# Three stages of a graph network kernel run with shorter lags between their steps

## The chip, the cores and the metric

One core of a Trainium2 chip runs the whole program in one launch. The metric is the device time of that launch in microseconds. Lower is better.

## The reference

Fifty thousand nodes of 128 features pass through four graph layers (a two-layer GCN, a three-layer GraphSAGE, an attention layer with a GRU, a summing layer), each followed by a residual sum and a layer norm. The parts that the change touches are these (biases left out):

```python
# GCN, second half: h is the scaled table of the first half
x1 = layernorm(x + dinv * segment_sum(h[src], dst) + ...)
# GraphSAGE, third layer, and what the attention layer asks of its output
x2 = layernorm(x1 + inv_deg * segment_sum(v[src], dst) + rest)
message = x2 @ W_msg + b_msg ;  score = x2 @ W_att ;  gh_n = x2 @ W_hh_n.T
# last layer
x4 = layernorm(x3 + segment_sum(x3[src], dst) @ W_neigh.T + x3 @ W_self.T + b)
```

## The kernel before

The nodes are cut into T = 98 groups of 512. The program is a row of stages, each of which walks over all 98 groups and writes a table to HBM that the next stage reads; every stage ends with a barrier, so the next one starts only when the last store has landed. The stages in question are gcn_second (its tiles are g2_*, shown as g_* in the profile), sage_third (s3_*, shown as s_*) and combine (cb_*).

Inside such a stage every engine runs its own program. `over_groups(eng, [(lag, stage), ...])` writes it: at step s the engine carries out, in the order of the list, each stage for group s - lag. The waits inside a stage block the engine (or the queue of SyncE, "SP", which issues the plain loads and stores), so everything that stands later in the list, or in later steps, stays behind them.

The work on one group g of sage_third is: DVE copies the row indices (`aim`, lag 0); GpSimd issues 3 to 5 indirect gathers of 128 rows each, 4.24 on average; DVE makes the one-hot matrices (`prepare`); PE multiplies rows by one-hots (`sums`); ACT copies the sum (`catch`); PE transposes it (`flip`); ACT scales it (`weight`); DVE adds the row block `s_rest` and takes the statistics (`add`, L1863); ACT takes the root (`root`); DVE inverts it (`invert`); ACT normalises (`apply`); PE transposes (`turn`); ACT copies (`hold`); PE multiplies (`message`), first 2 matmuls for `hx`, then 8 for the messages; ACT copies `hx` (`note`); DVE adds the bias to the messages (`bias`, writes `s_mout` and `s_asks`, L1874 and L1876). gcn_second ends with `apply`, and combine has a `dense` product in place of `flip`. On DVE the lags in the lists count from `prepare`, which itself runs four steps behind `aim`: `on_vector` adds 4 to each.

SP loads and stores for sage_third: `s_rest` (two buffers; the load of group g first waits until `add` of group g - 2 is done), `x2t` (after `hold`), `hxt` (after `note`), `t_m` and `asks_d` (both after `bias`). The store helper and the load helper are:

```python
def load(sp, q, to, what, loaded, free=None, slots=2):
    if free is not None and not (isinstance(q.t, int) and q.t < slots):
        wait_for(sp, free, q.t - (slots - 1))
    sp.dma_start(to, what).then_inc(loaded, 16)

def store(sp, q, to, what, made, stored):
    wait_for(sp, made, q.t + 1)
    sp.dma_start(to, what).then_inc(stored[q.d % len(stored)], 16)
```

The rows that are gathered lie in a ring of eight groups: `aim` of group s waits until `sums` of group s - 6 (or s - 7) is done.

Of the kernel before, what the change touches and what calls it, by code (L numbers as in the profile page):

```python
# [23 lines left out]
BLK = 4  # L24
GRP = BLK * P
T = -(-NODES // GRP)
NPAD = T * GRP
# [156 lines left out]
def build_program(nc, x, src, dst, w1, b1, w2, b2, ws0, wn0, sb0, ws1, wn1, sb1, ws2, wn2, sb2,  # L184
# [782 lines left out]
# [3 lines that stand above are left out]
# [444 lines left out]
    def gcn_second():  # L1414

        with ExitStack() as ctx:
            ph = Phase(ctx, "g2")
            e = EdgeRows(ph, t_h0, D)
            agg = ph.pair("agg", [P, GRP])
            ln = LayerNorm(ph)  # L1420
            rest, z, xout = ph.pair("rest", [P, GRP], n=4), ph.pair("z", [P, GRP], n=4), ph.pair("xout", [P, GRP])
            held, turned = ph.sem("held"), ph.sem("turned")
            loaded, added, stored = ph.sems("loaded", 4), ph.sem("added"), ph.sems("stored")
            scaled, weighted = ph.pair("scaled", [P, GRP]), ph.sem("weighted")
            block = ctx.enter_context(nc.Block())

            @block.gpsimd
            def _(pool):
                e.fetch(pool)

            @block.sync
            def _(sp):
                over_groups(sp, [
                    (3, lambda q: load(sp, q, rest[q.r][:, :], group_of(r1, q.t), loaded[q.r], added, 4)),
                    (9, lambda q: store(sp, q, group_of(t_x1[0:NPAD, :], q.t), xout[q.u][:, :], ln.applied,
                                        stored))])
                all_stored(sp, stored)

            @block.tensor
            def _(pe):  # L1440
                def sums(q):
                    e.fetched(pe, q)
                    if not is_first(q.t):
                        pe.wait_ge(held, q.t - 1)
                    e.sum_by_feature(pe, q, [bank[q.u]]).then_inc(e.summed, 1)

                def turn(q):
                    pe.wait_ge(held, q.t + 1)
                    if not is_first(q.t):
                        pe.wait_ge(weighted, q.t - 1)  # L1450
                    for b in range(BLK):
                        last = pe.transpose(bank[2 + q.u][:, b * P:(b + 1) * P],
                                            agg[q.u][:, b * P:(b + 1) * P], ident[:, :])
                    last.then_inc(turned, 1)

                over_groups(pe, [(3, turn), (1, sums)])

            @block.scalar
            def _(act):
                def hold(q):  # L1460
                    act.wait_ge(e.summed, q.t + 1)
                    if not is_first(q.t):
                        act.wait_ge(turned, q.t - 1)
                    act.activation(planes(agg[q.u]), nodes(bank[q.u]), ACT.Copy).then_inc(held, 1)

                def weight(q):
                    act.wait_ge(turned, q.t + 1)
                    if not is_first(q.t):
                        act.wait_ge(added, q.t - 1)
                    for b in range(BLK):  # L1470
                        last = act.activation(scaled[q.u][:, b * D:(b + 1) * D],
                                              bank[2 + q.u][:, b * D:(b + 1) * D], ACT.Copy,
                                              scale=col(dinv_n, q.t * BLK + b))
                    last.then_inc(weighted, 1)

                def apply(q):
                    if not is_first(q.t):
                        act.wait_ge(stored[q.u], q.n * 16)
                    ln.normalise(act, q, xout[q.u], z[q.r])

                over_groups(act, [(2, hold), (4, weight), (6, lambda q: ln.root(act, q)), (8, apply)])

            @block.vector
            def _(dve):
                def add(q):
                    dve.wait_ge(weighted, q.t + 1)
                    dve.wait_ge(loaded[q.r], q.m * 16 + 16)
                    if not is_first(q.t, 4):
                        dve.wait_ge(ln.applied, q.t - 3)
                    dve.tensor_tensor(z[q.r][:, :], scaled[q.u][:, :], rest[q.r][:, :], ALU.add)\  # L1490
                       .then_inc(added, 1)
                    dve.wait_ge(added, q.t + 1)
                    ln.take_stats(dve, q, z[q.r])

                e.on_vector(dve, [(7, lambda q: ln.invert(dve, q)), (5, add), (0, lambda q: e.prepare(dve, q))])


    def sage_first():
# [243 lines left out]
    def sage_third():  # L1742


        with ExitStack() as ctx:
# [18 lines left out]
            @block.sync  # L1764
            def _(sp):
                over_groups(sp, [
                    (4, lambda q: load(sp, q, rest[q.u][:, :], group_of(r2, q.t), loaded[q.u], added)),
                    (11, lambda q: store(sp, q, slab_of(x2t, q.t), xt[q.u][:, :], held, st_x)),
                    (13, lambda q: store(sp, q, slab_of(hxt, q.t), hx[q.u][:, :], noted, st_h)),
                    (13, lambda q: store(sp, q, group_of(t_m[0:NPAD, :], q.t), mout[q.u][:, :], biased, st_m)),  # L1770
                    (13, lambda q: store(sp, q, asks_d[bass.ds(q.t, 1), :].rearrange("o (p b) -> (o p) b", b=BLK),
                                         asks[q.u][:, :], biased, st_a))])
                all_stored(sp, st_x, st_m, st_a, st_h)

            @block.tensor
            def _(pe):
# [35 lines left out]
                                         skip_group_check=True)  # L1812
                    last.then_inc(timed, 1)

                over_groups(pe, [(3, flip), (1, sums), (11, message), (9, turn)])

            @block.scalar
            def _(act):
                def catch(q):
                    act.wait_ge(e.summed, q.t + 1)  # L1820
                    if not is_first(q.t):
                        act.wait_ge(flipped, q.t - 1)
                    act.activation(planes(agg[q.u]), nodes(bank[q.u]), ACT.Copy).then_inc(caught, 1)

                def weight(q):
                    act.wait_ge(flipped, q.t + 1)
                    if not is_first(q.t):
                        act.wait_ge(added, q.t - 1)
                    for b in range(BLK):
                        last = act.activation(scaled[q.u][:, b * D:(b + 1) * D],  # L1830
                                              bank[2 + q.u][:, b * D:(b + 1) * D], ACT.Copy,
                                              scale=col(inv_n, q.t * BLK + b))
                    last.then_inc(weighted, 1)

                def apply(q):
                    if not is_first(q.t):
                        act.wait_ge(turned, q.t - 1)
                    ln.normalise(act, q, x2[q.u], z[q.r])

                def hold(q):  # L1840
                    act.wait_ge(turned, q.t + 1)
                    if not is_first(q.t):
                        act.wait_ge(st_x[q.u], q.n * 16)
                        act.wait_ge(timed, q.t - 1)
                    act.activation(xt[q.u][:, :], bank[4][:, :], ACT.Copy).then_inc(held, 1)

                def note(q):
                    act.wait_ge(hidden, q.t + 1)
                    if not is_first(q.t):
                        act.wait_ge(st_h[q.u], q.n * 16)  # L1850
                    act.activation(hx[q.u][:, :], bank[5][:, :], ACT.Copy).then_inc(noted, 1)

                over_groups(act, [(2, catch), (12, note), (10, hold), (4, weight), (6, lambda q: ln.root(act, q)),
                                  (8, apply)])

            @block.vector
            def _(dve):
# [10 lines left out]
                def bias(q):  # L1868
# [4 lines left out]
                    for i in range(2):  # L1873
# [4 lines left out]
                                                 bm_r[:, :, :].rearrange("p b f -> p (b f)"), ALU.add)  # L1878
                    last.then_inc(biased, 1)

                e.on_vector(dve, [(12, bias), (7, lambda q: ln.invert(dve, q)), (5, add),
                                  (0, lambda q: e.prepare(dve, q))])


    def attend():
# [281 lines left out]
    def combine():  # L2167

        with ExitStack() as ctx:  # L2169
# [14 lines left out]
            def _(sp):  # L2184
                def leave(q):
# [3 lines left out]
                    else:  # L2189
# [3 lines left out]
                over_groups(sp, [  # L2193
                    (0, lambda q: load(sp, q, own_rows[q.u][:, :], own_group(t_x3, q.t),
                                       loaded[q.u], e.summed)),
                    (8, leave)])
                all_stored(sp, stored)

            @block.tensor
            def _(pe):  # L2200
# [20 lines left out]
                                         stop=True, skip_group_check=True)  # L2221
                    last.then_inc(dense_done, 1)

                over_groups(pe, [(1, sums), (3, dense)])

            @block.scalar
            def _(act):
# [9 lines left out]
                        act.wait_ge(stored[q.u], q.n * 16)  # L2237
                    ln.normalise(act, q, xout[q.u], z[q.r])

                over_groups(act, [(2, hold), (5, lambda q: ln.root(act, q)), (7, apply)])  # L2240

            @block.vector
            def _(dve):
# [7 lines left out]
                    dve.wait_ge(added, q.t + 1)  # L2251
                    ln.take_stats(dve, q, z[q.r])

                e.on_vector(dve, [(6, lambda q: ln.invert(dve, q)), (4, add), (0, lambda q: e.prepare(dve, q))])

    def if_general(*parts):

# [55 lines left out]
```

## Time and profile before

| | |
|---|---|
| time, median of 3 runs | 5544.67 us (5533.96 to 5554.54) |
| the profiled execution | 5548.76 us, span 5547.0 us |
| gcn_second, first gather to first gather of the next stage | 862.3 to 1420.3 us |
| sage_third, the same | 3409.2 to 3990.8 us |
| combine, first gather to the end | 5000.4 to 5547.0 us |

A row of the timeline reads: start, duration, engine, line, operation, tiles out<-in, shapes, how many, and in brackets how long the engine had been idle and what released it. "SPq" rows are DMA issues of SyncE's queue. The DMA share is the mean busy share of the 16 DMA engines.

### The profile page before, as it was taken

To read this page: it belongs to the slowest core of one execution; us is meant where nothing else is said; L and a number is where in the kernel's file an instruction comes from. 1 tells how busy PE (TensorE), PEld (TensorE's weight loads), DVE (VectorE), ACT (ScalarE), POOL (GpSimd) and SP (SyncE) were. 2 spreads that over 40 slices of the span, in tenths; PEclk is the share of its full clock that TensorE was granted. 3 is DMA by queue.
4 is the path that set the end of the run, shared out by engine and by line. 5 is a ranking of instruction groups with operands and counts; after the bars stand their busy time and mean duration, and the time that the engine had idled before them with its cause. 6 is when DMAs were issued, how large, how long until landed. Compare 5 with 4: busy or idle time off the path is not lost. (4 is left out here: it accounts for less than half of the span.)

```text
span 5547.0 us, 105377 instructions
## 1 busy us (share of the span) xinstructions
PE 4744.4 (86%) x27509; PEld 3749.1 (68%) x27509; DVE 3861.5 (70%) x11930; ACT 2782.1 (50%) x6703; POOL 3017.4 (54%) x2962
## 2 busy tenths in 40 slices
PE   4499996666799989999999997898799999447887
PEld 4488885555688867777777775777566666227887
DVE  8577775776688855555555554788688888885766
ACT  3644444656333322222222222788677777793545
POOL 0077765777677743333334333777466664007776
PEclk9999998777899989999999998999899999558999
DMA  4889994554577754444444443788877775784554
GB/s 149 274 246 275 273 270 142 151 147 147 177 237 238 236 170 151 153 154 150 150 147 153 152 153 92 223 250 249 245 221 222 222 225 181 261 294 132 153 148 141
DMA packets 551178, 1075.23 MB, mean 194 GB/s; under 512 B 110995, under 2 KB 118202, under 8 KB 547962
## 3 DMA queue, kind: packets, MB, share of 16 engines
q1 hardware_dynamic: 451194, 854.46, 46.5%
q0 software_dynamic: 99840, 219.14, 16.0%
q8 instruction: 55, 0.90, 0.1%
q14 instruction: 89, 0.73, 0.0%
HBM read 712.24 MB, written 360.98 MB: 193 GB/s over the span
## 5 line engine op out<-in xcount | busy, mean ns | idle before, releaser
L841 POOL DMA_INDIRECT s_rows<-t_h,s_index x416 | 525.4, 1263 | 831.5 <-DVE s_index L834 730.5
L841 POOL DMA_INDIRECT cb_rows<-t_x,cb_index x416 | 395.7, 951 | 451.4 <-DVE cb_index L834 327.7
L841 POOL DMA_INDIRECT g_rows<-t_x,g_index x416 | 425.9, 1024 | 384.9 <-issue 366.5
L841 POOL DMA_INDIRECT at_rows<-t_m,at_index x416 | 435.6, 1047 | 299.1 <-DVE at_index L834 189.8
L841 POOL DMA_INDIRECT s_rows<-t_v,s_index x416 | 405.1, 974 | 211.4 <-issue 120.4
L841 POOL DMA_INDIRECT s_rows<-t_x,s_index x416 | 420.5, 1011 | 154.8 <-issue 117.9
L841 POOL DMA_INDIRECT g_rows<-t_h,g_index x416 | 403.1, 969 | 171.1 <-issue 124.7
L905 PE MATMUL bank<-s_onehot,s_hi 128*128 128x80 f32 (+9 forms) x1758 | 436.7, 288 | 48.8 <-DVE s_lo L876 26.6
L1724 DVE TENSOR_TENSOR s_rout<-bank,s_x 128x512 f32<-128x512 f32 x98 | 67.9, 693 | 587.1 <-PE bank L1668 587.1
L905 PE MATMUL bank<-g_onehot,g_rows 128*128 128x80 f32 (+9 forms) x1172 | 299.6, 420 | 199.5 <-DMA g_rows<-t_h,g_index 193.5
L905 PE MATMUL bank<-s_onehot,s_lo 128*128 128x80 f32 (+9 forms) x1758 | 431.0, 285 | 0.0
L905 PEld LDWEIGHTS bank<-g_onehot,g_rows 128*128 128x128 f32 x1172 | 248.8, 243 | 253.8 <-issue 164.6
L1691 ACT ACTIVATE s_hid<-bank,sb_c 128x512 f32<-128x512 f32 x196 | 124.1, 684 | 568.3 <-PE bank L1656 568.3
L1668 PEld LDWEIGHTS bank<-wuv_s,s_hid 128*128 128x128 f32 x3136 | 365.5, 192 | 47.4 <-issue 47.4
L869 DVE TENSOR_SCALAR s_onehot<-iota,dcol 128x276 fp32r<-128x276 f32 (+15 forms) x1248 | 389.5, 376 | 0.5
L905 PEld LDWEIGHTS bank<-s_onehot,s_hi 128*128 128x128 f32 x1758 | 340.9, 194 | 57.4 <-issue 56.2
L1656 PE MATMUL bank<-s_ht,ws_s 128*128 128x512 f32 x784 | 368.8, 593 | 0.0
L1656 PE MATMUL bank<-s_agg,wn_s 128*128 128x512 f32 x784 | 368.4, 592 | 0.0
L1668 PE MATMUL bank<-wuv_s,s_hid 128*128 128x128 f32 x3136 | 366.0, 275 | 0.9 <-DVE s_rout L1724 0.9
L864 ACT ACTIVATE s_hi<-s_rows 128x640 fp32r<-128x640 f32 (+1 forms) x196 | 172.6, 881 | 375.0 <-DMA s_rows<-t_x,s_index 351.1
L905 PEld LDWEIGHTS bank<-s_onehot,s_lo 128*128 128x128 f32 x1758 | 341.5, 194 | 0.3 <-issue 0.2
L905 PE MATMUL bank<-cb_onehot,cb_rows 128*128 128x80 f32 (+9 forms) x1172 | 244.5, 363 | 84.9 <-DMA cb_rows<-t_x,cb_index 77.9
(334 smaller groups left out, 13011.1 us busy)
## 6 DMA issues: line engine op xcount, KB each, us to landing
s_scale<-inv_d SPq DMA_DIRECT2D x196, 256.0 KB
t_h<-s_hout SPq DMA_DIRECT2D x98, 512.0 KB
s_own<-t_h SPq DMA_DIRECT2D x98, 512.0 KB
t_m<-s_mout SPq DMA_DIRECT2D x98, 264.0 KB
at_own<-t_m SPq DMA_DIRECT2D x98, 264.0 KB
t_x<-so_x SPq DMA_DIRECT2D x98, 256.0 KB, 4.7
g_own<-t_x SPq DMA_DIRECT2D x98, 256.0 KB
g_scale<-dinv_d SPq DMA_DIRECT2D x98, 256.0 KB
```

The costliest lines, as they stand in the source:

```text
L841: pool.indirect_dma_start(out=self.rows[:, self.ring(q) + k, :], out_offset=None, in_=self.table[0:NPAD, :], in_offset=bass.IndirectOffset ...
L864: act.activation(self.hi[:, a:b, :], self.rows[:, a:b, :], ACT.Copy).then_inc(self.split, 1)
L869: last = dve.tensor_scalar(self.onehot[:, k, 0:WIDE[k]], iota[:, 0:WIDE[k]], col(dcol, q.m * K + k), None, ALU.is_equal)
L905: last = pe.matmul(to[:, a:b], part[:, at, h * P:(h + 1) * P], self.onehot[:, k, off:off + b - a], start=(i + s == 0), stop=(close and i + ...
L1656: last = pe.matmul(bank[4 + o][:, :], w[:, h, o * P:(o + 1) * P], r[q.u][:, h, :], start=(k + h == 0), stop=(k + h == 2))
L1668: last = pe.matmul(bank[6 + w][:, b * D:(b + 1) * D], hid[q.u][:, h, b * P:(b + 1) * P], wuv_s[:, h, w * D:(w + 1) * D], start=(h == 0), s ...
L1691: last = act.activation(hid[q.u][:, h, :], bank[4 + h][:, :], ACT.Relu, bias=sb1_c[:, h:h + 1])
L1724: dve.tensor_tensor(rout[q.u][:, :], bank[6][:, :], xin[q.u][:, :], ALU.add)\
```

## The change

Only the numbers and the order in the lists of steps change, in three stages. No instruction is added or taken away, no buffer changes its size, and no wait changes its condition.

```diff
@@ gcn_second
-                    (9, lambda q: store(sp, q, group_of(t_x1[0:NPAD, :], q.t), xout[q.u][:, :], ln.applied,
+                    (6, lambda q: store(sp, q, group_of(t_x1[0:NPAD, :], q.t), xout[q.u][:, :], ln.applied,
-                over_groups(pe, [(3, turn), (1, sums)])
+                over_groups(pe, [(1, sums), (2, turn)])
-                over_groups(act, [(2, hold), (4, weight), (6, lambda q: ln.root(act, q)), (8, apply)])
+                over_groups(act, [(2, hold), (4, lambda q: ln.root(act, q)), (3, weight), (5, apply)])
-                e.on_vector(dve, [(7, lambda q: ln.invert(dve, q)), (5, add), (0, lambda q: e.prepare(dve, q))])
+                e.on_vector(dve, [(0, lambda q: e.prepare(dve, q)), (4, lambda q: ln.invert(dve, q)), (3, add)])
@@ sage_third
                     (4, lambda q: load(sp, q, rest[q.u][:, :], group_of(r2, q.t), loaded[q.u], added)),
-                    (11, lambda q: store(sp, q, slab_of(x2t, q.t), xt[q.u][:, :], held, st_x)),
-                    (13, lambda q: store(sp, q, slab_of(hxt, q.t), hx[q.u][:, :], noted, st_h)),
-                    (13, lambda q: store(sp, q, group_of(t_m[0:NPAD, :], q.t), mout[q.u][:, :], biased, st_m)),
-                    (13, lambda q: store(sp, q, asks_d[bass.ds(q.t, 1), :].rearrange("o (p b) -> (o p) b", b=BLK),
+                    (7, lambda q: store(sp, q, slab_of(x2t, q.t), xt[q.u][:, :], held, st_x)),
+                    (9, lambda q: store(sp, q, slab_of(hxt, q.t), hx[q.u][:, :], noted, st_h)),
+                    (9, lambda q: store(sp, q, group_of(t_m[0:NPAD, :], q.t), mout[q.u][:, :], biased, st_m)),
+                    (9, lambda q: store(sp, q, asks_d[bass.ds(q.t, 1), :].rearrange("o (p b) -> (o p) b", b=BLK),
                                          asks[q.u][:, :], biased, st_a))])
-                over_groups(pe, [(3, flip), (1, sums), (11, message), (9, turn)])
+                over_groups(pe, [(6, turn), (1, sums), (2, flip), (7, message)])
-                over_groups(act, [(2, catch), (12, note), (10, hold), (4, weight), (6, lambda q: ln.root(act, q)),
-                                  (8, apply)])
+                over_groups(act, [(2, catch), (8, note), (4, lambda q: ln.root(act, q)), (3, weight), (5, apply),
+                                  (6, hold)])
-                e.on_vector(dve, [(12, bias), (7, lambda q: ln.invert(dve, q)), (5, add),
-                                  (0, lambda q: e.prepare(dve, q))])
+                e.on_vector(dve, [(0, lambda q: e.prepare(dve, q)), (4, lambda q: ln.invert(dve, q)), (3, add),
+                                  (8, bias)])
@@ combine
-                    (8, leave)])
+                    (6, leave)])
-                over_groups(pe, [(1, sums), (3, dense)])
+                over_groups(pe, [(1, sums), (2, dense)])
-                over_groups(act, [(2, hold), (5, lambda q: ln.root(act, q)), (7, apply)])
+                over_groups(act, [(2, hold), (4, lambda q: ln.root(act, q)), (5, apply)])
-                e.on_vector(dve, [(6, lambda q: ln.invert(dve, q)), (4, add), (0, lambda q: e.prepare(dve, q))])
+                e.on_vector(dve, [(0, lambda q: e.prepare(dve, q)), (4, lambda q: ln.invert(dve, q)), (3, add)])
```

Two places of sage_third, first the queue of SP at the head of the stage. The number behind a tile is its buffer (group modulo 2). Before, from the load of group 4 to the load that follows the first store of `asks_d`:

```order
L965 DMA s3_rest0<-r2 128x512
L965 DMA s3_rest1<-r2 128x512
L965 DMA s3_rest0<-r2 128x512
L965 DMA s3_rest1<-r2 128x512
L969 DMA x2t<-s3_xt0 128x512
L965 DMA s3_rest0<-r2 128x512
L969 DMA x2t<-s3_xt1 128x512
L965 DMA s3_rest1<-r2 128x512
L969 DMA x2t<-s3_xt0 128x512
L969 DMA hxt<-s3_hx0 128x512
L969 DMA t_m<-s3_mout0 128x528
L969 DMA asks_d<-s3_asks0 128x4
```

The next row there is the load of group 10. Of the change, from the load of group 2:

```order
L965 DMA s3_rest0<-r2 128x512
L965 DMA s3_rest1<-r2 128x512
L969 DMA x2t<-s3_xt0 128x512
L965 DMA s3_rest0<-r2 128x512
L969 DMA x2t<-s3_xt1 128x512
L965 DMA s3_rest1<-r2 128x512
L969 DMA x2t<-s3_xt0 128x512
L969 DMA hxt<-s3_hx0 128x512
L969 DMA t_m<-s3_mout0 128x528
L969 DMA asks_d<-s3_asks0 128x4
L965 DMA s3_rest0<-r2 128x512
```

The last row is the load of group 6. So ten loads of `s_rest` stood ahead of the stores of group 0, and now six do: behind the stores of group g comes the load of group g + 6, where it was that of group g + 10.

Second, DVE at the same place. `s3_z` has four buffers (group modulo 4), `s3_mout` two. Before, `bias` of group 0 and what follows it in the same step:

```order
L1874 COPY s3_asks0<-bank6 128x2
L1876 TENSOR_TENSOR s3_mout0<-bank6,bm_r 128x264
L1874 COPY s3_asks0<-bank7 128x2
L1876 TENSOR_TENSOR s3_mout0<-bank7,bm_r 128x264
L948 RECIPROCAL s3_ln_rstd1<-s3_ln_std1 128x4
L950 SCALAR_TENSOR_TENSOR s3_ln_shift1<-s3_ln_mv1,s3_ln_rstd1 128x4
L1863 TENSOR_TENSOR s3_z3<-s3_scaled1,s3_rest1 128x512
```

Of the change, the end of `bias` of group 0 and the next step up to its `add`:

```order
L1876 TENSOR_TENSOR s3_mout0<-bank7,bm_r 128x264
L834 COPY s3_index5<-idx 128x5
L869 TENSOR_SCALAR s3_onehot<-iota,dcol 128x312
L869 TENSOR_SCALAR s3_onehot<-iota,dcol 128x328
L869 TENSOR_SCALAR s3_onehot<-iota,dcol 128x344
L869 TENSOR_SCALAR s3_onehot<-iota,dcol 128x224
L869 TENSOR_SCALAR s3_onehot<-iota,dcol 128x344
L948 RECIPROCAL s3_ln_rstd1<-s3_ln_std1 128x4
L950 SCALAR_TENSOR_TENSOR s3_ln_shift1<-s3_ln_mv1,s3_ln_rstd1 128x4
L1863 TENSOR_TENSOR s3_z2<-s3_scaled0,s3_rest0 128x512
```

Before, `bias` of group 0 stood in one step with `add` of group 7, and `add` of group 10 came three steps later. Now `add` of group 6 is the first `add` behind `bias` of group 0.

## Rows read from the trace of the kernel before

**Rows 1.** Windows, three stages and the middle of one: start:end, length, busy of each engine, PEclk, DMA share, GB/s

```profile
859.00:1461.00 602.00, 376.17 (x1692) 318.12 (x1693) 395.91 (x1743) 322.80 (x992) 434.39 (x448) 0.76 0.48 140
3407.00:3990.00 583.00, 495.21 (x2936) 410.11 (x2936) 456.12 (x2082) 422.87 (x1176) 405.14 (x416) 0.95 0.79 225
4984.00:5547.00 563.00, 461.29 (x3144) 427.55 (x3144) 375.02 (x1742) 276.88 (x718) 395.67 (x416) 0.92 0.50 144
...
3530.00:3930.00 400.00, 363.17 (x2213) 303.39 (x2214) 347.63 (x1577) 317.81 (x885) 304.92 (x313) 0.99 0.87 247
```

**Rows 2.** Gathers by tile: ns min/median/max, first and last start

```profile
L841 POOL DMA_INDIRECT g_rows<-t_h,g_index x416: 940/944/1459, 862.3 to 1390.9; - x139
L841 POOL DMA_INDIRECT s_rows<-t_v,s_index x416: 940/944/1431, 3409.2 to 3939.8; - x139
L841 POOL DMA_INDIRECT cb_rows<-t_x,cb_index x416: 940/944/1114, 5000.4 to 5521.6; - x139
```

**Rows 3.** Waits of sage_third: us in total, times, longest us

```profile
POOL s_rows L841 <- issue: 120.4, 395, 0.3
DVE s_asks L1874 <- DMA asks_d<-s_asks: 38.6, 39, 3.0
SPq L105 <- DVE s_z L1863: 194.7, 79, 10.4
SPq L969 <- DVE s_mout L1876: 5.6, 5, 2.2
```

**Rows 4.** Timeline of sage_third near its middle, DVE and SP

```profile
3665.00 0.15 DVE L834 COPY s_index<-idx 128x4 uint32 x1
3665.06 0.15 DVE L1874 COPY s_asks<-bank 128x2 f32<-128x2 f32 x1
3665.53 0.42 DVE L1876 TENSOR_TENSOR s_mout<-bank,bm_r 128x264 f32<-128x264 f32 x1
3665.87 0.16 DVE L948 RECIPROCAL s_ln_rstd<-s_ln_std 128x4 f32<-128x4 f32 x1
3666.18 0.69 DVE L1863 TENSOR_TENSOR s_z<-s_scaled,s_rest 128x512 f32<-128x512 f32 x1
3667.11 0.35 SPq L965 DMA_DIRECT2D s_rest<-r  x1
...
3668.48 1.46 DVE L869 TENSOR_SCALAR s_onehot<-iota,dcol 128x328 f32<-128x328 f32 x4
3668.74 0.33 SPq L969 DMA_DIRECT2D t_m<-s_mout  x1
3669.32 0.33 SPq L969 DMA_DIRECT2D asks_d<-s_asks  x1
...
3675.91 0.16 DVE L1874 COPY s_asks<-bank 128x2 f32<-128x2 f32 x1 [0.58 <-DMA asks_d<-s_asks]
```

**Rows 5.** DMA issues: KB each, median us from issue to landing

```profile
g_rest<-r SPq DMA_DIRECT2D x98, 256.0 KB, 3.3
r<-s_rout SPq DMA_DIRECT2D x98, 256.0 KB, 2.0
at_x<-x2t SPq DMA_DIRECT2D x98, 256.0 KB, 4.3
at_hx<-hxt SPq DMA_DIRECT2D x98, 256.0 KB, 3.4
```

**Rows 6.** Timeline, head of sage_third: sums of group 6

```profile
3449.83 2.63 PE L905 MATMUL bank<-s_onehot,s_rows 128*128 128x112 f32 x14
```

**Rows 7.** Timeline, end of sage_third

```profile
3971.14 0.16 DVE L1874 COPY s_asks<-bank 128x2 f32<-128x2 f32 x1 [0.98 <-PE bank L1810]
...
3984.27 0.16 DVE L1874 COPY s_asks<-bank 128x2 f32<-128x2 f32 x1 [2.02 <-DMA asks_d<-s_asks]
...
3990.35 0.38 DVE L834 COPY at_index<-idx 128x5 uint32<-128x5 uint32 x4 [5.18 <-PEq L276]
```

**Rows 8.** Timeline, end of gcn_second, ACT

```profile
1399.73 0.60 ACT L1464 ACTIVATE g_agg<-bank 128x512 f32<-128x512 f32 x1 [3.31 <-PE bank L905]
...
1414.70 1.65 ACT L957 ACTIVATE g_xout<-g_z,g_ln_shift,g_ln_rstd 128x128 f32<-128x128 f32 x4 [0.48 <-DMA t_x<-g_xout]
```

**Rows 9.** Timeline, end of combine

```profile
5528.20 0.60 PE L2208 MATMUL bank<-ident,cb_own 128*128 128x128 f32 x4
...
5530.68 0.60 ACT L2232 ACTIVATE cb_agg<-bank 128x512 f32<-128x512 f32 x1 [2.00 <-PE bank L2220]
...
5542.23 1.65 ACT L957 ACTIVATE cb_xout<-cb_z,cb_ln_shift,cb_ln_rstd 128x128 f32<-128x128 f32 x4 [0.50 <-DMA out_dram<-cb_xout]
```

**Rows 10.** Timeline of sage_third near its middle, PE and ACT

```profile
3673.73 1.06 PE L1805 MATMUL bank<-s_xt,whh_s 128*128 128x512 f32 x2
3674.63 1.06 PE L1810 MATMUL bank<-wm_s,s_xt 128*128 128x132 f32 x8
3674.92 0.60 ACT L1851 ACTIVATE s_hx<-bank 128x512 f32<-128x512 f32 x1 [0.32 <-PE bank L1805]
3675.53 0.60 PE L1797 MATMUL bank<-ident,s_x 128*128 128x128 f32 x4
3675.96 0.60 PE L1788 MATMUL bank<-ident,s_agg 128*128 128x128 f32 x4
3676.80 1.14 ACT L1830 ACTIVATE s_scaled<-bank,inv_n 128x128 f32<-128x128 f32 x4
```

## The prediction

> **What bounds the kernel now.** I read the windows by stage first. In gcn_second, sage_third and combine no engine is busy for its whole stretch [rows 1], so I went to the gathers. Each of the three stages issues 416 of them, of 0.944 us by their median [rows 2], and behind each GpSimd idles 0.3 us for nothing but its own issue [rows 3]. That is 1.247 us a gather, 5.29 us for the 4.24 gathers of a group, and 517.5 us from the first gather to the last. The stages take 528.6, 530.6 and 521.2 us for it [rows 2]: 11, 13 and 4 us more. So all three are paced by GpSimd's issue, to within 1 to 3 per cent. What a shorter lag can save is then the end of a stage, when the gathers are out and the steps behind them run off, and at most those 28 us. What it can cost is that another chain becomes slower than 5.4 us a group, so I looked for the chains that close on themselves in each stage. The reader should look at sage_third: DVE and PE are busy there for 456 and 495 of 583 us, and the DMA engines for 0.79 of the time [rows 1]. It is the only stage of the three in which DVE waits for a store, `asks_d` [rows 3].
>
> **What the change moves.** The number of steps behind the gathers falls; the work per group stays.
>
> *The queue of SP in sage_third is where the change acts most.* SP is in order. The load of `s_rest` for group g stands at SP step g + 4, before and after. It is preceded by the stores of step g + 3. Before, these are the messages of group g - 10, which `bias` makes on DVE at step (g - 10) + 16 = g + 6, and `add` of group g, which needs the load, is at DVE step g + 9. After the change they are the messages of group g - 6, made on DVE at step (g - 6) + 12 = g + 6, as the last thing in that step, and `add` of group g is at DVE step g + 7. So the load waits behind a store that waits for DVE, and DVE needs the load one step later. Before, SP was let go by `add` (194.7 us of its waits) and hardly ever by `s_mout` (5.6 us) [rows 3]; the load left 10 us ahead of its use and DVE never waited for it. The two order listings show it: the load that follows `asks_d` of group 0 is that of group 10 before, of group 6 now.
>
> This closes a loop of one step, whose length is the pace of the stage if it exceeds 5.4 us. From the rows of the middle of the stage:
>
> - `add` with its statistics, 3666.18 to 3668.48: 2.30 us [rows 4]
> - `bias`, 3665.06 to 3665.95: 0.89 us [rows 4]
> - from the end of an `add` TENSOR_TENSOR that SP waits for (3666.87) to the issue (3667.11): 0.25 us, which I take for `bias` to the issue of `t_m` [rows 4]
> - `t_m` to `asks_d`, 3668.74 to 3669.32: 0.58 us, and as much again to the load [rows 4]
> - L, from the issue of the load to its landing.
>
> That is 4.60 us + L. DVE has only the index copy, 1.35 us of one-hots (4.24 at 0.3 to 0.4 us) and 0.3 us of `invert` beside it, about 2.0 us against 1.41 + L.
>
> L is not in the trace, since nobody waits for this load. Neighbours: 256 KB loads of the same kind land after 3.3 us in gcn_second (`g_rest`), and 3.4 (`at_hx`, the third of three DMAs issued in a row) and 4.3 us (`at_x`) in attend [rows 5]. The worst is the small `asks_d` store in the middle of this very stage: issued at 3669.32, released at 3675.91, 6.6 us [rows 4], in a stretch with the DMA engines 0.87 busy [rows 1]; at a slower pace they would be less loaded. I take 3.4 us, because `at_hx` too stands behind two others and its stage is about as loaded as this one would be. The lowest landing of any 256 KB DMA in the trace is the 2.0 us of a store (`r<-s_rout`) [rows 5]; for this load I take 2.6 as the low end, between that and 3.3, and keep 6.6 as the high one.
>
> The Trainium skill, "DMA: Bandwidth & Descriptors", section "Anatomy of one DMA — SWDGE (gpsimd) path", fits a DMA as about 2.0 us plus bytes / 436e3; for 256 KB that is an estimate of 2.6 us, L at its low bound, and the sum below would be 5686. The neighbours of this trace, 3.3 to 4.3 us, stand above it. The same section says that DMA engines never wait for a semaphore, the issuing sequencer does, before dispatch. The trace agrees (SP waits 194.7 us on DVE), and it speaks against this change.
>
> The loop is 4.60 + 3.4 = 8.0 us. When does it run? The first stores of messages go at SP step 9, the load of group 6 behind them, `add` of group 6 at DVE step 13, and so through `add` of group 97 at step 104: 92 steps. `bias` of group 0 at step 12 follows `sums` of group 6, which end at 3452.5 [rows 6]; with 2.5 us through ACT to the `add` of that step, 2.3 and 0.9 us on DVE, it ends near 3458. `bias` of group 92 ends 92 × 8.0 = 736 us later. Five `bias` steps remain; the last four before took 3984.27 - 3971.14 = 13.1, 3.3 each: 16.4 us. From the end of the last `bias` (3985.2) to the next stage 5.2 us pass [rows 7]. The next stage starts at 3458 + 736 + 21.6 = 4215.6 instead of 3990.35: **+225 us**. The stage's own shorter tail is in that number.
>
> *Other chains of sage_third.* With `bias` last in DVE's step there is a second loop over two steps: end of `bias`, 0.25 to release, `message` to `turn` 0.90, `turn` to `flip` 0.43, `sums` 2.3 (12 matmuls), `flip` 0.43, first two matmuls of `message` to `note` 1.19, `note` to the end of `weight` 1.7, `add` 2.30, `bias` 0.89 [rows 4, 10]: 10.4 us, 5.2 a step. That is just under the gathers' 5.29, and well under 8.0: hidden at no cost. If PE's clock fell to its lower level throughout, its 5 us would double and the loop give 7.7, still hidden.
>
> *gcn_second and combine.* Their SP lists have one load and one store. In gcn_second `rest` has four buffers, and the store before the load of group g is that of group g - 4 (ACT step g + 1), with `add` at DVE step g + 7: several groups of slack. In combine the load of group g follows the store of g - 7, let go by ACT step g - 2 as before. Per step both keep the gathers' pace: DVE and PE have 1.3 us or more to spare in gcn_second, and in combine the product of the group before needs only ACT's copy, made while `sums` of the next group run. I cost these at nothing; if ACT's copy came late, PE would stand still for up to its 1.1 us a step, of which 0.6 is slack, 50 us in all.
>
> Their ends get shorter. gcn_second: the last copy of a sum starts at 1399.73, the last `apply` ends at 1416.35 [rows 8]. Now `weight` of group 96 (1.0) follows the copy and `add` of 96 that, from 1401.5; ACT then has `weight` of 97 and `apply` of 95, which ends near 1406.7. Its store lands 3.5 us later, and only then may `apply` of 97 start, at 1410.2, to end at 1411.9: **-4.5**. combine: the last transposes end at 5528.8, but the copy waits for the product of group 95 until 5530.68, and `apply` ends at 5543.9 [rows 9]. Now the product of 95 is done before `sums` of 97, so the copy starts 1.8 us earlier. `add` of 96 runs from about 5530.7 and `add` of 97 behind it to 5535.3; `root`, `invert` and two `apply` of 1.65 in the row at the end, partly beside `add`, bring it to about 5537.9: **-6**.
>
> **Sum.** 225 - 4.5 - 6 = +214.5 us. Against the profiled execution (5548.76) it is 5763; against the median shown (5544.67, 4 lower) 5759. I give 5760, 3.9 per cent slower.
>
> **The rivals.**
>
> *A. The load lands in time; the kernel gets faster.* If SP reached the load early enough, the stages would keep the gathers' pace, sage_third would lose three `bias` steps from its end (9.8 us) and the 13 us by which it trails its gathers (the loop through `asks_d` gets shorter), with the 10.5 of the other two: 5511. It needs 1.41 + L under 2.0 us, L under 0.6, and the shortest neighbour is 3.3. Chance 0.04.
>
> *B. The load is mostly hidden and the second loop decides.* At a lower granted clock (between the 0.76 and 0.95 that stages show [rows 1], PE's 5 us times 1.2) it is 11.3 / 2 = 5.65 us: 3479.6 + 92 × 5.65 = 3999.4, +9, less 10.5: 5543, no change. Against it stands the same L. Chance 0.05.
>
> *C. The DMA queues stay as full as now*, because each step still moves the same bytes and the load is issued right behind 264 KB of messages: L is 6.6, the step 11.2, the stage ends at 4510, the time is 6053. For it: the 6.6 us of `asks_d` in this stage. Against: the gathers would come half as often. Chance 0.10.
>
> *D. The forecast*, L between 2.6 and 4.6: steps of 7.2 to 9.2, 5686 to 5870. Chance 0.81.
>
> **How the numbers follow.** The range is that of D, a little widened for the ends of the stages: 5680 to 5880; it leaves out A, B and C, 0.19. Half a per cent (28 us) is about what a measurement of this kernel can tell. Slower: C and D, 0.91; same: B, 0.05; faster: A, 0.04.
>
> **What would show it.** In the changed profile the waits of sage_third should hold a row "DVE s_z <- DMA s_rest" of some 92 times and 250 us, absent before. SP's waits should move from `s_z` to `s_mout`. One step (from `add` to `add`) should be 8 us, gathers should idle for `s_index` some 2.7 us a group, and the next stage should start near 4215. gcn_second and combine should show the same distance from first to last gather and ends 4 to 6 us shorter. It is wrong if `add` finds its load landed, or if L is outside 2.6 to 4.6.

## The result, and the profile after

The changed kernel takes 5838.27 us, median of 6 runs (5831.4 to 5846.46), against 5547.48 us before (6 runs, 5533.96 to 5554.54): a ratio of 1.053, 95% interval 1.0519 to 1.0541. It is 5.3 per cent slower; 3.9 were forecast. The profiled execution has a span of 5836.4 us, 289.4 more than before.

The windows by stage come first (columns as in [rows 1]; the last line is the middle of sage_third):

```profile
860.00:1409.00 549.00, 342.89 (x1564) 291.59 (x1564) 374.01 (x1688) 324.67 (x980) 401.00 (x417) 0.78 0.49 143
3398.00:4280.00 882.00, 589.85 (x2936) 479.02 (x2936) 436.88 (x2080) 444.63 (x1176) 405.20 (x416) 0.86 0.49 148
5295.00:5836.00 541.00, 457.53 (x3132) 426.17 (x3132) 377.49 (x1686) 265.63 (x686) 394.07 (x416) 0.93 0.51 146
3530.00:4200.00 670.00, 450.18 (x2258) 366.86 (x2258) 333.66 (x1594) 342.11 (x901) 311.59 (x320) 0.87 0.48 150
```

DVE is busy in sage_third for 437 us (456 before) and GpSimd for 405 (405 before), but the stage is 300 us longer, and the DMA share fell from 0.79 to 0.49. The gathers by tile, as in [rows 2], and the first of attend, which follows sage_third:

```profile
L841 POOL DMA_INDIRECT g_rows<-t_h,g_index x416: 938/944/1450, 859.2 to 1386.5; - x139
L841 POOL DMA_INDIRECT s_rows<-t_v,s_index x416: 938/944/1454, 3399.0 to 4199.6; - x139
L841 POOL DMA_INDIRECT at_rows<-t_m,at_index x416: 938/1012/1455, 4286.7 to 4970.4; - x139
L841 POOL DMA_INDIRECT cb_rows<-t_x,cb_index x416: 940/944/1103, 5295.2 to 5814.8; - x139
```

From first gather to first gather of the next stage, sage_third takes 887.7 us where it took 581.6: +306.1. gcn_second (its next stage starts at 1409.0) takes 549.8 instead of 558.0, -8.2; combine, from its first gather to the end, 541.2 instead of 546.6, -5.4. The rest, -3.1, lies ahead of gcn_second and in stages that were not changed. These make the 289.4.

The waits of sage_third in the changed kernel (us in total, times, longest), to set beside [rows 3]:

```profile
DVE s_z L1863 <- DMA s_rest<-r: 386.6, 92, 5.2
POOL s_rows L841 <- DVE s_index L834: 373.3, 79, 85.0
PEld bank L1810 <- DVE s_mout L1876: 350.4, 97, 5.6
...
SPq L105 <- DVE s_mout L1876: 389.6, 80, 5.9
```

The wait of DVE for the load was absent before. It comes 92 times, once in each step of the loop that the prediction drew, and SP is now let go by `s_mout` where it was let go by `s_z`. PE and GpSimd wait for DVE, which waits for the load. GpSimd's 373.3 us hold one wait of 85.0 for the start of the stage; the rest is 2.9 us a group, 2.7 forecast. The timeline shows one turn, DVE and then SP:

```profile
3704.65 0.42 DVE L1876 TENSOR_TENSOR s_mout<-bank,bm_r 128x264 f32<-128x264 f32 x1
...
3706.41 0.16 DVE L950 SCALAR_TENSOR_TENSOR s_ln_shift<-s_ln_mv,s_ln_rstd 128x4 f32<-128x4 f32 x1
3710.53 0.69 DVE L1863 TENSOR_TENSOR s_z<-s_scaled,s_rest 128x512 f32<-128x512 f32 x1 [3.96 <-DMA s_rest<-r]
...
3713.37 0.42 DVE L1876 TENSOR_TENSOR s_mout<-bank,bm_r 128x264 f32<-128x264 f32 x1
...
3705.31 0.33 SPq L969 DMA_DIRECT2D t_m<-s_mout  x1
3705.89 0.33 SPq L969 DMA_DIRECT2D asks_d<-s_asks  x1
3706.49 0.35 SPq L965 DMA_DIRECT2D s_rest<-r  x1
...
3714.03 0.33 SPq L969 DMA_DIRECT2D t_m<-s_mout  x1
```

`bias` ends at 3705.07, and the messages leave 0.24 us later. The load leaves 1.18 us behind them, and `add` can start only 4.04 us after that. DVE's own work beside it was done at 3706.57. The step from store to store is 8.72 us. Over the whole loop, `add` of group 5 starts at 3445.20 and that of group 97 at 4261.18: 8.87 us a step. The landing of the load, which [rows 5] could not show for lack of a waiter, has a number now (DMA issues of 3530 to 4200 us: count, KB, median us to landing):

```profile
s_rest<-r SPq DMA_DIRECT2D x75, 256.0 KB, 4.2
```

It is 4.25 us as a mean over the last 88 pairs of a load's issue and the start of the `add` that waited for it. All landings called L below are made in this way.

### The profile page after: what moved, and what is told of

The parts are those of the page before. It is cut to its first block and busy times, and to the rows that moved or that the text cites. A ratio compares the mean times of both kernels' runs of the same rounds, so it can differ in the third digit from the quotient of the medians.

```text
span 5836.4 us, 105386 instructions
## 1 busy us (share of the span) xinstructions
PE 4832.2 (83%) x27509; PEld 3817.4 (65%) x27509; DVE 3854.5 (66%) x11930; ACT 2813.2 (48%) x6703; POOL 3018.2 (52%) x2962
## 5 line engine op out<-in xcount | busy, mean ns | idle before, releaser
L841 POOL DMA_INDIRECT s_rows<-t_v,s_index x416 | 405.2, 974 | 481.3 <-DVE s_index L834 373.3
L1810 PE MATMUL bank<-wm_s,s_xt 128*128 128x132 f32 x784 | 144.0, 339 | 270.3 <-DVE s_mout L1876 270.3
L1810 PEld LDWEIGHTS bank<-wm_s,s_xt 128*128 128x128 f32 x784 | 121.1, 232 | 351.4 <-DVE s_mout L1876 350.4
```

The lines of the kernel that those rows point to most:

```text
L841: pool.indirect_dma_start(out=self.rows[:, self.ring(q) + k, :], out_offset=None, in_=self.table[0:NPAD, :], in_offset=bass.IndirectOffset ...
L1810: last = pe.matmul(bank[6 + b // 2][:, (b % 2) * MW:(b % 2 + 1) * MW], xt[q.u][:, b * P:(b + 1) * P], wm_s[:, :], start=True, stop=True, s ...
```

## The experiments

The runs fall into three sets, each with its own runs of the kernel before; a ratio is the time over that of the kernel before in the same set, with its 95% interval. In the first set (s3_as_before, rest_lag2, old_lag7, four_buffers) the kernel before itself took 6618.12 us (17 runs). In the second (rest_lag2, old_lag7 and four_buffers again, and load_first) it took 5548.18 (9 runs), in the third (rest_lag3, s3_as_before again, load_between, bias_first) 5547.21 (13 runs). The sums were made for a kernel of 5547 us, so only the second and third sets are held against them. Why the first was slow is not known; the last section has what is known of it. The changed kernel itself was measured once, with the result, and a difference to its 5838 us compares two sets.

**1. gcn_second and combine as changed, sage_third as before.** The lists of steps of `sage_third` are those with a minus in the diff.

> The change in gcn_second and combine only; sage_third keeps its old lags and order. Theory (the loss is the loop through the load of s_rest in sage_third, the rest of the change is a small gain at two stage ends): 5530 to 5540 against 5547, no wait of DVE for s_rest. Rival (shorter lags cost each of the three stages something): above 5547, with more idle time of GpSimd for its indices in gcn_second or combine than the 1 to 2 us there now.

6595.62 us against 6618.12, ratio 0.9959 (0.9934 to 0.9984). Again:

> gcn_second and combine as changed, sage_third as before. From the traces of the two kernels gcn_second ends 8 us sooner and combine 5 us sooner (first gather to next stage or end): 5547 - 13 = 5534 us; by the prediction's own terms 5547 - 10.5 = 5537. If the order inside the steps costs anything in these stages, 5547 or more.

5532.28 us (9 runs) against 5547.21, ratio 0.9974 (0.9964 to 0.9984), 14.9 us less. So the whole loss comes from the edits in sage_third, and the gain of the two others is about what their traces say (13.6 us). The waits for `s_rest` are gone with the old lists.

**2. The load two places earlier in SP's queue**, in the changed kernel:

```diff
-                    (4, lambda q: load(sp, q, rest[q.u][:, :], group_of(r2, q.t), loaded[q.u], added)),
+                    (2, lambda q: load(sp, q, rest[q.u][:, :], group_of(r2, q.t), loaded[q.u], added)),
```

> The whole change, and in addition the load of s_rest in SP's list of sage_third at lag 2 instead of 4, so that it stands behind the stores of group g - 8 and not g - 6. Theory: the loop is gone, sage_third is paced by its gathers again (about 5.3 us a group) and its end is shorter, 5510 to 5530 in all. Rival B (the loop over bias, message, sums, weight and add is the next bound, 5.65 us a group or more): 5545 to 5600.

In the first set 6678.23 us, ratio 1.0096 (1.0063 to 1.013). The waits for `s_rest` were gone, and yet the kernel was 1 per cent slower than the kernel before: DVE waited 306.7 us in sage_third for `s_ln_std`, in 43 waits, and the gathers no longer set the pace. So the first expectation failed there, and why is not settled. Again in the second set:

> The same kernel as rest_lag2 (the whole change with the load of s_rest at lag 2). The first time every kernel of the set ran near 6600 us, with gaps inside PE's and ACT's own streams in all stages, so that nothing was paced by the gathers. Where the kernel before runs near 5547 again: theory 5510 to 5530, gathers 5.3 us a group in sage_third, no wait of DVE for s_rest. Rival B (the loop over bias, message, sums, weight and add is the next bound): 5545 to 5600.

5516.46 us (5 runs), ratio 0.9939 (0.9926 to 0.9953): as expected. All the rest of the change is in this kernel, all its lags and orders; one number in SP's list takes away 322 us of the 5838.

**3. The same load one place earlier** (lag 3).

> The changed kernel with the load of s_rest one place earlier in SP's queue (lag 3 for 4), behind the messages of group g - 7 instead of g - 6. Theory: the loop then spans two steps, 8.9 / 2 = 4.4 us a step, under the 5.3 of the gathers: 5510 to 5530 us, as with lag 2, no DVE waits for s_rest. Rival (each step of lag takes away only part of the wait, in proportion): halfway between 5838 and 5516, 5677 us.

5511.43 us (4 runs, 5507.82 to 5517.16), ratio 0.9936 (0.992 to 0.9951). One step of slack is enough, as a loop of one step would have it; the rival, a loss in proportion to the lag, put it at 5677. This is as fast as experiment 2 within the measurement, and both beat both kernels. Its waits in sage_third:

```profile
POOL s_rows L841 <- issue: 122.0, 400, 0.3
PEld bank L1810 <- DVE s_mout L1876: 93.1, 78, 2.7
POOL s_rows L841 <- DVE s_index L834: 89.5, 16, 85.0
```

GpSimd idles for its own issue 400 times (395 in [rows 3]), and for `s_index` hardly anywhere but at the start of the stage (85.0 of 89.5 us). Its gathers and the next stage's first:

```profile
L841 POOL DMA_INDIRECT s_rows<-t_v,s_index x416: 940/944/1389, 3395.2 to 3920.1; - x139
L841 POOL DMA_INDIRECT at_rows<-t_m,at_index x416: 938/972/1457, 3961.3 to 4645.2; - x139
```

The stage takes 566.1 us instead of 581.6, 15.5 less: 5.7 between its first and last gather, 9.8 at its end.

**4. The kernel before, with the load moved back in SP's queue** (lag 7 for 4), so that it stands behind the messages of group g - 7. Nothing of the change is in it.

```diff
-                    (4, lambda q: load(sp, q, rest[q.u][:, :], group_of(r2, q.t), loaded[q.u], added)),
+                    (7, lambda q: load(sp, q, rest[q.u][:, :], group_of(r2, q.t), loaded[q.u], added)),
```

> The kernel before with one number changed: the load of s_rest at lag 7 instead of 4 in SP's list of sage_third. It then stands behind the stores of group g - 7, which bias makes early in the DVE step whose add needs the load. Theory: the old order too gets a loop of one step, bias 0.89 + 1.41 + landing 4.2 + add 2.3 + one-hots 1.35 + index 0.15 = 10.3 us a group, for 91 groups: about 5990. Rival (the slowdown of the change comes from the order on DVE, PE or ACT, the load only shows it): 5547, unchanged.

6840.77 us, ratio 1.0343 (1.0286 to 1.0401) in the first set, and again:

> The same kernel as old_lag7 (the kernel before, the load of s_rest at lag 7). Where the kernel before runs near 5547: theory, a loop of one step of 0.89 + 1.41 + 4.2 + 2.3 + 1.5 = 10.3 us a group, about 5990. Rival (the cause lies in the lists of DVE, PE or ACT): 5547.

5918.24 us, ratio 1.0666 (1.0646 to 1.0685). The load's place alone makes such a loss in the old kernel. The time is 72 us less than I expected: the step is 9.47 us, since L is 3.66 and not 4.2 and the one-hots cost less than I put in. The waits of the stage:

```profile
DVE s_z L1863 <- DMA s_rest<-r: 449.7, 93, 8.0
POOL s_rows L841 <- DVE s_index L834: 422.5, 80, 85.0
```

**5. Four buffers for `s_rest` instead of two**, in the changed kernel (shortened: `loaded` has four semaphores, and `add` waits for and reads the buffer of the group modulo 4):

```diff
-            rest, z, x2 = ph.pair("rest", [P, GRP]), ...
+            rest, z, x2 = ph.pair("rest", [P, GRP], n=4), ...
-                    (4, lambda q: load(sp, q, rest[q.u][:, :], group_of(r2, q.t), loaded[q.u], added)),
+                    (4, lambda q: load(sp, q, rest[q.r][:, :], group_of(r2, q.t), loaded[q.r], added, 4)),
```

> The whole change, and s_rest with four buffers in place of two (its load waits for add of group g - 4), its place in SP's list unchanged at lag 4. Theory (place in the queue behind the stores, not the buffers): unchanged, 5838 within 15 us. Rival (the load is held back by the buffer that add must free): the time falls to about 5520.

6737.13 us, ratio 1.0187 (1.0132 to 1.0242), and again:

> The same kernel as four_buffers (the whole change with four buffers of s_rest, its load still at lag 4). Where the kernel before runs near 5547: theory 5838 within 15 us, since the load still stands behind the stores. Rival (the buffer holds it back): about 5520.

5853.6 us (2 runs, 5846.63 to 5860.57), ratio 1.0549 (1.053 to 1.0568). That is 15 us above the changed kernel, just outside what I had allowed, and nowhere near 5520; the two sets show 92 and 93 waits for `s_rest`, as the changed kernel does. The buffers are not what holds the load. More of them do not help a load that stands behind another's wait.

**6. The load ahead of both stores, released by the same `bias`.** In the changed kernel the load first waits for `bias` of group g - 6, as it does now by way of the queue, and then leaves ahead of the messages:

```diff
+                def fetch_rest(q):
+                    if not isinstance(q.t, int) or q.t >= 6:
+                        wait_for(sp, biased, q.t - 5)
+                    load(sp, q, rest[q.u][:, :], group_of(r2, q.t), loaded[q.u], added)
...
-                    (4, lambda q: load(sp, q, rest[q.u][:, :], group_of(r2, q.t), loaded[q.u], added)),
...
+                    (3, fetch_rest),
                     (9, lambda q: store(sp, q, group_of(t_m[0:NPAD, :], q.t), mout[q.u][:, :], biased, st_m)),
```

> The whole change, but the load of s_rest for group g still waits for bias of group g - 6 and is then issued ahead of the stores of t_m and asks_d instead of behind them. It measures what of the 4.2 us landing comes from standing behind the 264 KB of messages. If the landing is the same wherever it stands: the step is 2.30 + 0.89 + 0.25 + 4.2 = 7.65 us, 1.15 less than now, the time about 5732. If the stores ahead of it cost 0.8 us of landing (then it is the 3.4 of the forecast): 6.85 us a step, about 5660.

5640.77 us (2 runs), ratio 1.0166 (1.0147 to 1.0184), 19 us under the second number and far from the first. One turn in the trace, DVE and then SP (five lines were added, so `add` is at L1868 here):

```profile
3706.43 0.69 DVE L1868 TENSOR_TENSOR s_z<-s_scaled,s_rest 128x512 f32<-128x512 f32 x1 [2.51 <-DMA s_rest<-r]
...
3712.92 0.69 DVE L1868 TENSOR_TENSOR s_z<-s_scaled,s_rest 128x512 f32<-128x512 f32 x1 [2.15 <-DMA s_rest<-r]
...
3710.02 0.35 SPq L965 DMA_DIRECT2D s_rest<-r  x1
3710.63 0.33 SPq L969 DMA_DIRECT2D t_m<-s_mout  x1
3711.21 0.33 SPq L969 DMA_DIRECT2D asks_d<-s_asks  x1
```

L is 2.90 us here and 3.24 on the mean, 1.01 less than in the changed kernel. Two issues less (1.16) and a shorter L (1.01) make 2.17 us a step; measured are 8.87 - 6.75 = 2.12.

**7. The load between the messages and `asks_d`**, to see which of the two makes L longer:

```diff
-                    (4, lambda q: load(sp, q, rest[q.u][:, :], group_of(r2, q.t), loaded[q.u], added)),
...
                     (9, lambda q: store(sp, q, group_of(t_m[0:NPAD, :], q.t), mout[q.u][:, :], biased, st_m)),
+                    (3, lambda q: load(sp, q, rest[q.u][:, :], group_of(r2, q.t), loaded[q.u], added)),
                     (9, lambda q: store(sp, q, asks_d[bass.ds(q.t, 1), :]...
```

> The changed kernel with the load of s_rest issued between the messages (t_m) and the small asks_d store, instead of behind both. The load of the changed kernel lands 4.25 us after its issue; put ahead of both stores it landed after 3.24 us. If the 264 KB of messages ahead of it make the difference, L stays 4.25 and only one issue of 0.58 us leaves the loop: step 8.87 - 0.58 = 8.29 us, total 5838 - 53 = 5785 us. If the small asks_d store does (its packets are of 16 bytes), L falls to 3.24 as well: step 7.28, total 5838 - 146 = 5692 us. Between the two if both take part.

5683.62 us (4 runs), ratio 1.025 (1.0235 to 1.0266), L 3.14, step 7.15. The second of the two numbers came out. One turn, DVE and then SP:

```profile
3708.24 0.69 DVE L1863 TENSOR_TENSOR s_z<-s_scaled,s_rest 128x512 f32<-128x512 f32 x1 [1.98 <-DMA s_rest<-r]
...
3704.84 0.33 SPq L969 DMA_DIRECT2D t_m<-s_mout  x1
3705.44 0.35 SPq L965 DMA_DIRECT2D s_rest<-r  x1
3706.04 0.33 SPq L969 DMA_DIRECT2D asks_d<-s_asks  x1
```

The load leaves 0.60 us behind 264 KB of messages, and `add` starts 2.80 us later. The 264 KB directly ahead did not lengthen L (3.24 without them, experiment 6). Moving the 2 KB of `asks_d` from behind the load to ahead of it makes 1.1 us of difference in this kernel. By what means is not shown, and the last section has a case against `asks_d` alone.

**8. `bias` first in DVE's step instead of last**, in the changed kernel:

```diff
-                e.on_vector(dve, [(0, lambda q: e.prepare(dve, q)), (4, lambda q: ln.invert(dve, q)), (3, add),
-                                  (8, bias)])
+                e.on_vector(dve, [(8, bias), (0, lambda q: e.prepare(dve, q)), (4, lambda q: ln.invert(dve, q)),
+                                  (3, add)])
```

> The changed kernel with the bias at the head of DVE's step instead of at its end; the queue of SP and every lag stay as changed. Theory (a loop of one step, add, bias, store issues, load, add): the bias of a step now stands ahead of the one-hots and the add of the same step, so a load that it lets go is wanted only by the add of the next step; the loop of 8.87 us spans two steps, 4.4 us a step, under the 5.3 of the gathers, and the kernel runs in 5510 to 5540 us with next to no waits of DVE for s_rest. Rival (the place of the load in SP's queue costs by itself, whatever DVE's order): 5838 us, step 8.9.

5636.33 us (4 runs), ratio 1.0157 (1.0142 to 1.0173): neither number. Two thirds of the loss are gone, but `add` still waits for the load 57 times, 158 us. What holds SP now is another store, that of `x2t` (DVE, then ACT, then SP):

```profile
3703.01 0.69 DVE L1863 TENSOR_TENSOR s_z<-s_scaled,s_rest 128x512 f32<-128x512 f32 x1 [4.74 <-DMA s_rest<-r]
...
3715.26 0.69 DVE L1863 TENSOR_TENSOR s_z<-s_scaled,s_rest 128x512 f32<-128x512 f32 x1 [2.58 <-DMA s_rest<-r]
...
3705.39 0.21 ACT L942 ACTIVATE s_ln_std<-s_ln_var 128x4 f32<-128x4 f32 x1 [5.73 <-DVE s_ln_var L937]
...
3706.57 1.65 ACT L957 ACTIVATE s_x<-s_z,s_ln_shift,s_ln_rstd 128x128 f32<-128x128 f32 x4
3708.10 0.60 ACT L1845 ACTIVATE s_xt<-bank 128x512 f32<-128x512 f32 x1
...
3708.95 0.33 SPq L969 DMA_DIRECT2D x2t<-s_xt  x1
...
3711.39 0.35 SPq L965 DMA_DIRECT2D s_rest<-r  x1
```

ACT's list begins the step's later half with `root`, which waits for `add`, and ends it with `hold`, which makes `s_xt`. So the chain runs `add`, statistics, `root`, `weight`, `apply`, `hold`, the store of `x2t`, three more stores, the load, and the `add` after the next: 12.25 us for two steps, 6.1 us a step, which is still above the gathers' pace (the mean step of the last 88 is 6.72). SP was let go by `s_xt` for 304.5 us in 80 waits, and by `s_mout` for 4.5 us. My theory had looked only at the store that the load was known to wait for; every store ahead of it in the queue has a chain of its own. That this chain makes up the whole of the remaining loss was not tried by itself. Experiment 3 puts the load one place earlier and leaves no loss, but with `bias` last.

## Why the prediction was right, and its size too small

**The mechanism** was shown as the prediction put it: the same loop, its 92 steps, its waits (92 times; 386.6 us, 250 forecast), SP's waits moved to `s_mout` (389.6 us). Experiment 4 makes the loop without the change, experiments 2 and 3 take it away within the change, and experiment 5 excludes the buffers.

**The step that failed in size is the term L**, "I take 3.4 us". It is 4.25 us. The other terms hold: 4.60 + 4.25 = 8.85 against 8.87 measured. The sum also holds where L and the terms are changed. L is measured up to the start of `add`, so a sum that meets the step says that the loop has no slack in it and that the other terms stayed as they were; it does not test L.

| kernel | terms without L | L | sum | step measured |
|---|---|---|---|---|
| changed | 4.60 | 4.25 | 8.85 | 8.87 |
| four buffers | 4.60 | 4.44 | 9.04 | 9.09 |
| load first (two issues less) | 3.44 | 3.24 | 6.68 | 6.75 |
| load between (one less) | 4.02 | 3.14 | 7.16 | 7.15 |
| old, lag 7 (one-hots and index in the loop, 1.17) | 5.77 | 3.66 | 9.43 | 9.47 |

Measured steps are means over the last 88. The 1.17 is what lies longer between the start of `add` and the end of the next `bias` than in the changed kernel (4.37 and 3.20 us on the mean).

I chose 3.4 from `at_hx` [rows 5], "because at_hx too stands behind two others". That was misread. It is the third of three loads in the list, but in the trace of before only `at_own` (264 KB) leaves directly ahead of it, 0.51 us by the median; `at_x` leaves 5.64 us ahead. One turn:

```profile
4206.27 0.33 SPq L965 DMA_DIRECT2D at_x<-x2t  x1
4211.12 0.33 SPq L965 DMA_DIRECT2D at_own<-t_m  x1
4211.64 0.33 SPq L965 DMA_DIRECT2D at_hx<-hxt  x1
```

So `at_hx` is like the load of experiment 7, which stands directly behind 264 KB and has L at 3.14. It is not like the load of the changed kernel, which has `asks_d` between. The same row read rightly would not have given 4.25 either; none of [rows 5] is a large load directly behind a small store. The other half of my reasoning is not borne out: the DMA share did fall (0.87 to 0.48 in the middle), yet L was 4.25 at this share, and 3.14 at 0.71 in experiment 7 and 3.24 at 0.77 in experiment 6. That the time still landed in its range is partly luck: L came from an unlike neighbour, and 4.25 lies inside the 2.6 to 4.6 that I allowed.

**Point by point.** `bias` of group 0 ends 49.2 us after the first gather (3448.22 less 3399.0), 48.8 forecast (3458 less 3409.2). 92 steps take 816 us, 736 forecast: this is the whole difference of +306 and +225 in the stage. The last five `bias` take 16.6 us (4264.23 to 4280.81), 16.4 forecast, and 5.25 us more to the next stage, 5.2 forecast.

gcn_second keeps its distance from first to last gather (527.3 for 528.6) and its end is 6.9 us shorter (29.4 to 22.5), 4.5 forecast. My sum let the last `apply` wait for its buffer until a store had landed. It did not wait:

```profile
1393.97 0.60 ACT L1464 ACTIVATE g_agg<-bank 128x512 f32<-128x512 f32 x1 [2.03 <-PE bank L905]
...
1401.87 3.17 ACT L957 ACTIVATE g_xout<-g_z,g_ln_shift,g_ln_rstd 128x128 f32<-128x128 f32 x8
```

From the last copy of a sum to the end of the last `apply` are 11.1 us, 16.6 before [rows 8]. combine ends 3.8 us sooner behind its last gather, 6 forecast, and 5.4 sooner in all. Together 13.6 us by the traces, and 14.9 (0.16 to 0.36 per cent of 5547) by experiment 1's times; 10.5 forecast. sage_third's new lists are a gain as well once the loop is gone: 15.5 us by the trace of experiment 3.

**The rivals.** A gave 5511 if the load lands in time; experiments 2 and 3, in which it does, ran in 5516 and 5511. Its split was half right: the 9.8 us at the end are there, the gathers gained 5.7 us of 13. B needed the load to be nearly hidden, and it was not; its own loop, over `message`, `sums`, `weight` and `add`, did not show in experiment 3, which kept the gathers' pace. C had L at 6.6 since the queues stay as full; the longest L of the last 88 is 4.75 us. The rule of the Trainium skill, "DMA: Bandwidth & Descriptors", section "Anatomy of one DMA — SWDGE (gpsimd) path", 2.0 us plus bytes / 436e3, gives 2.6 us for 256 KB as an estimate; every mean L measured here is above it, 3.14 to 4.44 us. The page's fit is for DMAs that GpSimd issues, and these loads are SyncE's, with other traffic beside them. The same section's sentence that the issuing sequencer is what waits agrees with SP's 389.6 us on DVE.

## What to carry to other kernels

On an in-order queue a load inherits every wait of the stores ahead of it, whatever its own buffer would allow. When lags are cut, write down for each load which store stands ahead, which engine step lets that store go, and in which step the load is used. With one step between them the chain is a loop of one step and sets the pace if it is longer than the step (8.87 us here against 5.3). With two it may be twice as long, and here it cost nothing (experiment 3). Do this for every store ahead, not only for the last one (experiment 8). When the lags of a load's users are cut, cut the load's lag too. A small store directly ahead of a load that is waited for is worth a trial behind it (experiment 7).

## What was not expected of the hardware

- A 256 KB load directly behind a 2 KB store (`asks_d`, 128x4 f32) landed after 4.25 us on the mean; directly ahead of that store, with 264 KB of messages 0.6 us ahead, after 3.14. Both have gathers and further stores beside them. It is not the small store alone: in the old kernel with lag 7 it is ahead as well, and L was 3.66. There the next store (`x2t`) often comes later: L was 3.46 us in the 42 steps in which it was issued more than 4.5 us behind the load, 3.84 in the other 46, and 4.56 in the 7 of them in which it came within 2.5 us. But in the changed kernel, where `x2t` always comes within 2.9 us, its distance made hardly any difference (4.21 us in the 50 steps within 1.75 us, 4.30 in the other 38), nor did it with `asks_d` behind the load (3.15 and 3.12 us within and beyond 2.5). What lengthens L stays open.
- The granted clock of PE was 0.87 in the middle of the slower stage, where PE worked 0.67 of the time. It was 0.99 before [rows 1], at 0.91 of the time, and 1.00 in experiment 3, at 0.93. No term of the loop is work of PE, and PE waited for `s_mout`, so nothing here shows a cost of the lower clock.
- The kernel before took 6618.12 us in the first set of runs, 5548.18 in the second and 5547.21 in the third, and the lag-2 kernel changed sign between the first two (1.0096 and 0.9939). The first and the third set both ran on a chip numbered 8, the second on one numbered 0, so this is not shown to be a matter of the chip. In the first set the gathers of sage_third, with its old lists, took 713 us from first to last, and 536 in the third, for one and the same kernel. All four traces of the first set hold waits of ACT that the profile puts down to another core or an unknown queue, 695 to 1022 us over the whole program and up to 34.6 us each; the traces of the later sets hold none. The cause is open. The sign of a one per cent change in such a state need not hold outside it.
